# A two-branch transformer block on one core: the whole order of its 760 steps written out in one table

## The reference, cut to what matters

```python
xn = _layernorm(x)
x  = x + attn(xn) + ffn(xn)

# attn: heads of 8 channels, chunks of 16 tokens, once in order and once at a stride of 3 tokens
local_out  = _chunk_attention(xn, Wq, bq, Wk, bk, Wv, bv, 16)
atrous_out = the same on every third token
attn = (local_out + atrous_out) @ Wo.T + bo

# ffn: causal latent attention with 16 heads over all 512 tokens, then 8 experts
x1  = xn + mla(rmsnorm(xn))
ffn = x1 + moe(rmsnorm(x1))
# moe: shared expert + 7 routed experts; top 2 of sigmoid(xt @ W_router + routing_bias), their scores normalized;
# each expert: (silu(xt @ Wg) * (xt @ Wu)) @ Wd
```

## Time and profile before

| what | value |
|---|---|
| median of the runs | 391.2 us (389.04 to 397.37) |
| span of the profiled execution | 387.9 us |
| PE busy | 337.9 us, 87% |
| DVE busy | 286.0 us, 74% |
| ACT busy | 224.1 us, 58% |
| POOL busy | 122.7 us, 32% |
| mean granted TensorE clock | 0.984 |
| chain that ended last | PE 48%, DVE 28%, ACT 10%, issue 7%, SP's queue 3% |

### The profile page before, as it was taken

One profiled execution on the slowest core, in us unless ns is written; L12 is line 12 of the kernel. 1 busy time (PEld: TensorE's weight loads), 2 busy tenths in 40 slices (PEclk: granted clock), 3 DMA queues, 4 the chain that ended last, 5 costly groups with the idle time before them and its releaser, 6 DMA issues.

```text
span 387.9 us, 11664 instructions
## 1 busy us (share of the span) xinstructions
PE 337.9 (87%) x4504; PEld 205.0 (53%) x4504; DVE 286.0 (74%) x720; ACT 224.1 (58%) x545; POOL 122.7 (32%) x148
## 2 busy tenths in 40 slices
...
GB/s 193 82 197 100 26 155 43 89 56 65 27 22 160 24 69 54 84 167 3 64 41 30 58 65 48 43 6 161 3 2 0 3 0 27 3 28 0 30 0 27
DMA packets 29141, 21.84 MB, mean 56 GB/s; under 512 B 12312, under 2 KB 26008, under 8 KB 29048
## 3 DMA queue, kind: packets, MB, share of 16 engines
...
q10 hardware_dynamic: 216, 0.20, 0.2%
...
## 4 chain that ended last, share of the span: by engine, by line
PE 48%; DVE 28%; ACT 10%; issue 7%; SPq 3%; DMA 1%; ACTq 1%; POOL 1%; DVEq 0%; POOLq 0%
PE bank_B L1428 11%; DVE neg_max L1068 6%; PE bank_c L1332 6%; PE bank_A L1434 5%; PE bank_B L1236 5%; PE bank_A L1374 5%; ACT p_mla L886 3%; DVE s_loc L1085 2%; DVE row_max L1082 2%; ACT k_diag L830 2%; PE bank_M L1272 2%; SPq L624 1%; PE bank_M L1382 1%; DVE k_diag L1193 1%; PE bank_M L1397 1%
## 5 line engine op out<-in xcount | busy, mean ns | idle before, releaser
L886 ACT ACTIVATE p_mla<-bank_B 128x512 f32<-128x512 f32 (+1 forms) x176 | 94.3, 562 | 62.7 <-PE bank_B L1222 61.9
L1068 DVE TENSOR_REDUCE neg_max<-bank_A 128x1 f32<-128x512 f32 (+3 forms) x176 | 108.6, 637 | 19.5 <-PE bank_A L1222 15.8
L1236 PE MATMUL bank_B<-q_stack,k_stack 54*128 54x512 bf16 (+3 forms) x256 | 63.2, 303 | 10.9 <-DVE neg_max L1068 5.1
L1215 PE MATMUL bank_A<-k_stack,q_stack 52*128 52x512 bf16 (+3 forms) x256 | 63.7, 303 | 0.1
L1428 PE MATMUL bank_B<-xrT,k_diag 128*128 128x512 f32 x128 | 61.7, 600 | 1.2 <-DVE k_diag L1193 1.0
L759 POOL TENSOR_TENSOR x<-x,q_part 128x512 f32<-128x512 f32 x31 | 39.4, 1272 | 61.3 <-ACT q_part L920 43.0
L1332 PE MATMUL bank_c<-p_mla,v_mla 128*32 128x128 f32 (+12 forms) x512 | 47.5, 444 | 5.6 <-ACT p_mla L886 5.5
L1236 PEld LDWEIGHTS bank_B<-q_stack,k_stack 54*128 54x128 bf16 x256 | 19.2, 93 | 54.0 <-issue 23.1
L920 ACT ACTIVATE q_part<-bank_A,expert_w 128x128 f32<-128x128 f32 x108 | 30.8, 368 | 28.8 <-PE bank_A L1434 28.8
L1193 DVE SCALAR_TENSOR_TENSOR k_diag<-k_diag,bank_B 128x512 f32<-128x512 f32 x32 | 22.0, 687 | 31.5 <-ACT k_diag L904 30.3
L1222 PE MATMUL bank_A<-masks 64*128 64x64 bf16 (+2 forms) x352 | 43.1, 202 | 0.0
...
## 6 DMA issues: line engine op xcount, KB each, us to landing
v_dram<-v_rows SPq DMA_DIRECT2D x12, 324.0 KB, 3.6
...
```

Source lines behind the costliest of these rows:

```text
L886: drained_by(nc.scalar.activation(p_of(n)[:, m:m + len(heads), 0:w], src, ACT.Exp, scale=SCALE), step)
L1068: drained_by(nc.vector.tensor_reduce(neg_max[:, g, m:m + len(heads), i], src, AX.X, ALU.max, negate=True), step)
L1215: return nc.tensor.matmul(bank_of(step)[:, n * w:(n + 1) * w], q_stack[b % 2][rows, h % 8, i * P:(i + 1) * P], k_stack[b % 2][rows, h % 8, ...
L1236: nc.tensor.matmul(bank_of(step)[:, m * w:(m + 1) * w], k_stack[b % 2][rows, h % 8, j * P:(j + 1) * P], q_stack[b % 2][rows, h % 8, j * P: ...
```

## The change

The table `SPREAD`, the function `merged` and the rules that build the lists are gone. In their place stands `ORDER`, one text in which every step is a word (`KD.0.0`), and a star stands for the next pair of S and E, or for the next single one (`*3` for three). The 760 steps are the same, and no instruction that a step issues is changed; 656 of the 760 stand at another place of the list. The steps S, the steps E, and the steps of each batch in most kinds keep their order among themselves. A new assertion asks that ROUTE of a batch stands behind the whole PICK of the batch before.

```diff
--- before.py
+++ after.py
@@ -58,10 +58,8 @@
 PV_WIDTH = 32
 PT_RING = 1
 KD_PARTS = 4
-ST_PARTS = 8
 KD_FIRST = 2
 PICK_PARTS = 4
-OUTPUT_AT = 3
 
 WARM = {("WF",): 6, ("XT", 0, 1): 2, ("MA", 0, 0): 2, ("S", 0, 0): 10, **{("S", 0, n): 1 for n in range(2, 12)}}
 
-SPREAD = {
-    "scores": [(-0.544, 4.136)],
-    "local": [(-0.436, 0.411), (0.765, 1.39), (1.708, 2.786), (2.68, 3.494)],
-    "project": [(-0.445, -0.071), (0.596, 1.129), (1.381, 1.941)],
-    "stacks": [(-1.405, -1.405), (-0.092, 0.281), (1.13, 1.348), (1.807, 3.073)],
...
-def merged(*parts):
-
-    keyed = [(lo + (hi - lo) * (k + 0.5) / len(one), n, k, step)
-             for n, (one, lo, hi) in enumerate(parts) for k, step in enumerate(one)]
-    return [step for x in sorted(keyed, key=lambda x: x[:3]) for step in (x[3] if isinstance(x[3], list) else [x[3]])]
...
+ORDER = """
+LN.0 WF XT.0.1 MA.0.0 MB.0 MA.0.1 XT.0.0 ST.0.0 LK.0 LQ.0 STATS.1 ST2.0 MV.0 ROOT LV.0.0 KD.0.0 * KD.0.1 * KD.0.2
+LV.0.1 *3 KD.0.3 LN.1 *2 LV.0.2 XT.1.0 STATS.2 VD.0.0 LS.0.0 * LK.1 LR.0.0 LQ.1 *2 PT.0.0 * LS.0.1 * SHIFT.0.0
+LV.1.0 *2 LV.1.1 *2 LV.1.2 LO.0.0 *2 LR.0.1 PT.0.1 LT.0.0 LS.0.2 XT.1.1 LO.0.1 * MA.1.0 MB.1 VD.0.1 * MV.1 * LR.0.2
+MA.1.1 PT.0.2 LT.0.1 * LS.0.3 *4 ST.1.0 LO.0.2 * LR.0.3 PV.0.0.0 ST.1.1 ST.1.2 * ST.1.3 SHIFT.0.1 ST.1.4 ST.1.5
...
+DOWN.3.5 GU.3.7 DOWN.3.6 DOWN.3.7
+"""
...
 def plan():
 
...
-    lists = [(experts(range(B)), *at["experts"][0]), (scores(), *at["scores"][0])]
...
-    steps += merged(*lists)
+
+    groups = [(b, g) for b in range(B) for g in GROUP_ORDER]
+    maxima = [("S", b, n) for b in range(B) for n in range(H // 4 * PER_GROUP)]
+    exps = [("E", b, g, j, u) for b, g in groups for j in range(NT) for u in range(len(exp_units(g, j)))]
+    pairs = [[step for of, at in ((maxima, n), (exps, n - LEAD * PER_GROUP)) if 0 <= at < len(of) for step in of[at:at + 1]]
+             for n in range(len(maxima) + LEAD * PER_GROUP)]
+    steps, sent = [], 0
+    for word in ORDER.split():
+        if word[0] == "*":
+            count = int(word[1:] or 1)
+            steps += [step for pair in pairs[sent:sent + count] for step in pair]
+            sent += count
+        else:
+            kind, *of = word.split(".")
+            steps.append((kind, *(int(n) for n in of)))
+    assert sent == len(pairs) and len(set(steps)) == len(steps)
     at = {step: n for n, step in enumerate(steps)}
     assert at["KD", 0, KD_PARTS - 1] < at["LS", 0, 0]
+    assert all(at["PICK", b, PICK_PARTS - 1] < at["ROUTE", b + 1] for b in range(B - 1))
     assert at["ROOT",] < min(at["LN", 1], at["STATS", 2], at["R2", 0])
     assert all(at["STATS", b] < at["LN", b] for b in range(1, B))
     assert all(at["ROUTE", b] < at["PICK", b, 0] and at["PICK", b, PICK_PARTS - 1] < at["DOWN", b, 1] and at["X1", b] < at["R2", b] for b in range(B))
```

More of the change, by code:

```diff
@@ new lines @@
+ORDER = """
[3 more added lines that the diff above has]
+MA.1.1 PT.0.2 LT.0.1 * LS.0.3 *4 ST.1.0 LO.0.2 * LR.0.3 PV.0.0.0 ST.1.1 ST.1.2 * ST.1.3 SHIFT.0.1 ST.1.4 ST.1.5
+ST.1.6 *2 PT.0.3 *4 LT.0.2 SHIFT.0.2 PV.0.0.1 LS.0.4 PV.0.0.2 * PV.0.0.3 *2 LO.0.3 * LR.0.4 * Y.0.0 KD.1.0 PV.0.1.0
@@ new lines @@
+PT.0.4 *2 KD.1.1 LT.0.3 * LO.0.4 * PV.0.1.1 * PV.0.1.2 LT.0.4 * SHIFT.0.3 * PV.0.1.3 *3 KD.1.2 Y.0.1 *2 PV.0.2.0
+KD.1.3 *2 LN.2 PV.0.2.1 * VD.1.0 * LW.0 XT.2.0 PV.0.2.2 PV.0.2.3 *2 LK.2 *2 Y.0.2 LS.1.0 LQ.2 *2 SHIFT.1.0 LR.1.0
+LV.2.0 ST.1.7 *2 PT.1.0 LS.1.1 PV.0.3.0 LV.2.1 LV.2.2 *2 LO.1.0 LR.1.1 PV.0.3.1 * PT.1.1 LT.1.0 *2 PV.0.3.2 *
+SHIFT.1.1 LS.1.2 LO.1.1 VD.1.1 PV.0.3.3 XT.2.1 LR.1.2 * Y.0.3 PT.1.2 LT.1.1 LS.1.3 MA.2.0 MB.2 MA.2.1 * ST.2.0 YT.0
+ST.2.1 * LO.1.2 LR.1.3 X1.0 PV.1.0.0 *2 PT.1.3 LT.1.2 * KD.2.0 * PV.1.0.1 * LS.1.4 LO.1.3 SHIFT.1.2 *2 PV.1.0.2
```

100 lines of the change are left out of this document (19 added, 81 removed).

## The result

The changed kernel takes 373.24 us (median of four executions, 371.83 to 379.14), the kernel before 393.64 us (389.04 to 397.37, with one more execution than was known at first). The ratio is 0.9545, 95% interval 0.9456 to 0.9634: faster by 4.5%. The profiled execution takes 371.8 us, with a span of 369.6 us; before, the span was 387.9. The forecast of 384.5 us had the direction, and a third of the size: 6.6 us of span where 18.3 were gained.

The account below looks back on a forecast made before the run. It took PE and DVE both as near the bound, with only waiting able to change: 11.1 us of waits, 63% counted as 7.0, less 0.4, gave a 381.3 us span, plus 3.3, about 384.5 us; 8-in-10 range 375 to 395.

Parts of the forecast that it names:

- PV: PE's PV steps waiting for ACT's exponential, 5.3 us in 13 waits; 4.0 us expected to go.
- YT and X1: PE's waits before YT.1, X1.1 and X1.2 for DVE or ACT; all 2.8 us expected to go.
- The start: Steps up to LS.0.0: ACT freed sooner for k_diag, so LS.0.0 starts 2.0 us earlier; bounds 0 and 3.6.
- SP's queue: Transfers reordered so that E.0.3.0.0 and LS.3.0 no longer wait for SP; 2.3 us expected to go.
- The tail: GU.0.0 stands three score steps later, leaving waits for the last exponentials unfilled; 0.4 us lost.
- the share of 48 / (48 + 28) = 63%: PE's part of the chain among PE and DVE; scaled 11.1 us of removed waits to 7.0 us.
- The prediction's own sign for the share: Bank B's waits for neg_max and s_loc would tell if 63% was wrong: above 13 us or below 6.
- what was put at nothing: Moved-back SHIFT.0.1, ST.1.7 and expert weights, and ACT's price for later PV: no cost in the likeliest case.
- the first: Rival: waits on DVE shrink too, half of 8.8 us; gain 15.1 us, 376 us; chance 0.20.
- the second: Rival: every wait comes back behind DVE, only the start's last 1 us stays; 390 us; chance 0.14.
- The third's sign: Rival: p_mla's two buffers hold up ACT, about 400 us, chance 0.12; sign: ACT waits over 10 us for PV.
- The clock rival: New PE pauses drop TensorE's clock twice more for 3 us, up to 6 us lost; 390.5 us; chance 0.04.

Follow-up runs that it names:

- g4: The change's order with SHIFT.0.1 moved one pair earlier, ahead of ST.1.2; 374.29 us, ratio to before 0.9507.
- h3: The kernel before, with DVE's row maxima of S taking half of each head's columns (output differs); 386.31 us, ratio 0.9828.
- h4: The changed kernel, with DVE's row maxima of S taking half of each head's columns (output differs); 370.60 us, ratio to before 0.9408.
- g2: The order before, with PV, the chunk attention (LS, LR, PT, LO, LT, LW) and Y, YT, X1 at the change's places; 404.02 us, ratio 1.0313.
- f3: The order before, with only the chunk attention (LS, LR, PT, LO, LT, LW) at the change's places; 408.50 us, ratio 1.0388.
- f1: The order before, with only the 64 PV steps and two Y that must follow at the change's places; 400.71 us, ratio 1.0103.
- g1: The order before, with only Y, YT and X1 of the four batches at the change's places; 393.79 us, ratio 1.0051.
- f2: The change's order, with the 64 PV steps back at the score steps they had before; 384.68 us, ratio to before 0.9761.
- h1: The change's order up to S.2.0, then the order before for the steps left; 384.36 us, ratio to before 0.9750.
- h2: The order before up to S.2.0, then the change's order for the steps left; 388.67 us, ratio to before 0.9733.

## Why the prediction was right in sign and short in size

**The list of waits** forecast 11.1 us, and the measured fall was 11.6. That the two are so close is in part luck: the four terms that I named came to 8.8 us, and waits that I hadn't listed to most of the rest. Point by point:

- *PV*, 4.0 taken: 5.3 became 0.4, so 4.9. The bound was nearly reached.
- *YT and X1*, 2.8 taken: all three waits gone; YT.0 (0.7, behind MA's turned_q) and YT.2 (0.28) are new. Net 1.8.
- *The start*, 2.0 taken: the waits before LV.0.2 (2.28) and LS.0.0 (0.94) are gone, S.0.0's for its stacks (2.24) is new. Net 1.0; LS.0.0 starts at 33.28, 1.2 sooner, not 2.0, behind a new wait of 0.56 of XT.1.0, which is counted with the short ones below. I had named the DMAs as ACT's delay and not asked when they land.
- *SP's queue*, 2.3 taken: both waits gone. SHIFT.0.1, which I counted at nothing, is waited for 0.97 us. I had reckoned that PE comes there 2 us sooner and the transfers too; PE came 5 us sooner. By g4 the queue in front of it made a quarter of the wait at most. ST.1.7, S.3.0 and GU.0.0 did cost nothing. Net 1.1.
- *Not on the list*: the short waits in bank M and of LS that none of these terms names fell from 11.0 to 7.6 us. LT's went from 2.9 to 0.7, MA's from 2.4 to 1.0. No row of them was over 1.6 us in the view, and I passed over them all. 3.4 us, less the 0.4 that bank B's waits for DVE grew and 0.2 more.
- *The tail*, 0.4 lost: from S.3.43 on the change is 2.3 us faster.

**Two steps failed.** The forecast fell 11.7 us short, 6.6 for 18.3. The first step is what comes through, the share of 48 / (48 + 28) = 63%. It took DVE's part of the chain as work that stays when PE's waits go. By it 11.1 us became 7.0, which is 4.1 of the 11.7. In fact the waits fell by 11.6 in all, with what came back already taken off. h3 speaks against the share: had DVE been the second limit, 38 us off its 286 should have freed more than 6.8, and h4 shows it no closer to the limit in the new order. The prediction's own sign for the share, bank B's waits for DVE above 13 us or below 6, didn't catch this: they are 9.2.

The second step is what was put at nothing, by the sentence that only the waiting can change and by a list of the largest waits alone. That is most of the shortfall, 9.5 us: 3.7 by which the matmuls themselves took less, 1.7 of idle time ahead of 20 us, 1.3 in the experts' part and in gaps below the view's rows, and 2.8 net of unlisted waits. Against these the named terms came to 2.3 less than their 11.1, and the 0.4 of the tail wasn't lost. DVE's part of the chain is 28% in the change too, so that share doesn't tell what a wait on PE is worth.

**The rivals.** The time landed nearest the first, 376 us, but not by its mechanism: it asked for less than 6 us of bank B's waits for DVE, and they are 9.2. Nothing came back behind DVE as the second had it. The third's sign came, and its price didn't. ACT's waits in the changed kernel:

```profile
ACT p_mla L830 <- PE bank_B L1166: 31.0, 39, 3.7
ACT p_mla L830 <- PE bank_c L1276: 22.4, 15, 3.2
```

ACT waits 22.4 us for PV's buffers, where before it had no such row, and 31.0 instead of 59.7 for the scores. Its idle time changed owner, and PE waits 0.2 us for p_mla in bank B. The clock rival put 6 us on two more drops. In the attentions they came: the mean clock there is 0.97, where it was 0.99, and at the start it rose in exchange. Over the whole span it is 0.978 in the profiled execution (before 0.984), and 0.975 in the median (before 0.971). So the rival's event happened in part and its loss didn't: PE's busy time fell. In g2, f3 and f1 there was a loss, 10, 5 and 3 us by the table's last column.

What makes the clock differ between the orders stays open. Counting PE's idle gaps from 20 to 290 us in the profiled executions, before has 94, the change 61 and g2 73; of 1 us and more they have 5, 4 and 14. The Trainium skill, TensorE: Matmul & The Clock Gate, section A second HAM failure mode: psum-queue depth-cycling, puts such a swinging clock down to frequent micro-pauses between groups of matmuls. The case speaks against that as a count: before has the most gaps of the three and the highest clock, 0.984. Long gaps go with a low clock in g2 (0.945) and f3 (13 gaps of 1 us and more, 0.958), but h3 has nine and the highest clock of all, 0.991, and g4 and h4 have four each and 0.953 and 0.963. Over the 14 traces the correlation of the clock with the number of long gaps is only -0.46.

**What a sum over parts can't tell.** By kind, each of the moved kinds that were tried alone costs 0.5 (g1, hardly told from nothing) to 4.9%, and the whole gives 4.5%. R2, R3, X2T, ROUTE, PICK and GU were not tried alone. f1 and f2 fit one reason for PV: a later PV frees PE only where the steps around it are ready in its place. My sum took every removed wait as settled where it stood. In the whole change that held; in the kernels that moved one kind it did not. That the neighbours had moved as well is my reading of it, and no run isolates a neighbour. By stretch the gains nearly add up (h1, h2).

What stays open: which neighbours PV needs. g2 gave it the chunk attention and Y, YT and X1, and its idle time was still before's. Why the same matmuls take 3.7 us less in the change's profiled execution, at a clock no higher, isn't settled either; in g4's, with nearly the same order and a clock of 0.953, they took 341.2 us.
